# Context of the graph attention turned back by VectorE and DMA instead of TensorE, in a four-layer graph transformer on one core

## The reference

```python
h = jnp.maximum(_layernorm(x), 0.0);  x = x + attention(h, Wq, bq, Wk, bk, Wv, bv, Wf, bf, adj)
h = jnp.maximum(_layernorm(x), 0.0);  x = x + graph(h, adj, W, b, w_src, w_dst, H_w, H_b)

def graph(feat_in, adj, W, b, w_src, w_dst, H_w, H_b):     # 12 heads, 32 features each
    h = jnp.einsum('bnd,ade->bane', feat_in, W)
    th = jnp.tanh(h)
    attn = einsum('bane,aeo->bano', th, w_src) + swapaxes(einsum('bane,aeo->bano', th, w_dst), 2, 3)
    attn = jnp.where(attn >= 0, attn, 0.2 * attn)
    attn = softmax(jnp.where(~adj[:, None], -999.0, attn))
    feat_out = elu(heads_joined(jnp.einsum('banm,bame->bane', attn, h) + b))
    gate = sigmoid(feat_in @ H_w.T + H_b)
    return gate * feat_out + (1.0 - gate) * feat_in
```

## Time and profile before

| | |
|---|---|
| runs | 2123.85, 2126.32, 2125.83 us |
| the profiled execution | 2124.53 us, span 2122.7 us |
| TensorE matmuls, weight loads | busy 2035.4 us (96%), 1897.6 us (89%) |
| ScalarE, VectorE, GpSimd | busy 1954.5 (92%), 1779.6 (84%), 1570.1 us (74%) |
| granted TensorE clock | 0.991 of full speed over the span |
| DMA | 80.27 MB, mean 38 GB/s |

### The profile page before, as it was taken

The page is one execution under the profiler, slowest core; times in us unless marked ns, Lnnn a source line. Parts: engine busy times, 40 slices in busy tenths (PEclk is TensorE's granted clock), DMA queues, the critical chain, the costliest instruction groups (busy, mean ns, idle before and its releaser), DMA issues.

```text
span 2122.7 us, 58492 instructions
## 1 busy us (share of the span) xinstructions
PE 2035.4 (96%) x19980; PEld 1897.6 (89%) x19980; DVE 1779.6 (84%) x4117; ACT 1954.5 (92%) x6800; POOL 1570.1 (74%) x2874
## 2 busy tenths in 40 slices
PE   4999999999999999999999999999999999999985
PEld 3899889898899999999999999999999999999974
DVE  3688888888888888888888888888888888888876
ACT  3699899998999999999999999999999999999986
POOL 6467777777777777777777777777777777777765
PEclk9999999999999999999999999999999999999987
DMA  4001111111211000000320101001000010000000
GB/s 153 16 25 36 40 54 51 36 51 44 60 56 36 29 29 25 29 28 25 99 92 29 29 24 30 28 27 32 25 28 29 25 33 25 29 29 20 18 12 23
DMA packets 85983, 80.27 MB, mean 38 GB/s; under 512 B 22582, under 2 KB 85436, under 8 KB 85692
## 3 DMA queue, kind: packets, MB, share of 16 engines
q1 hardware_dynamic: 85692, 76.52, 11.8%
HBM read 44.26 MB, written 32.24 MB: 36 GB/s over the span
## 4 chain that ended last, share of the span: by engine, by line
PE 86%; POOL 8%; ACT 2%; issue 2%; DVE 1%; SPq 0%; DMA 0%; POOLq 0%; DVEq 0%; ACTq 0%
PE psum L718 36%; PE psum L728 18%; PE psum L710 5%; PE psum L796 5%; PE psum L807 4%; PE psum L818 4%; PE psum L784 3%; PE psum L854 2%; PE psum L741 2%; PE psum L836 2%; PE psum L750 2%; POOL prod L406 2%; PE psum L825 1%; POOL x L420 1%; POOL x L382 1%
## 5 line engine op out<-in xcount | busy, mean ns | idle before, releaser
L492 ACT ACTIVATE LG<-LG,neg_max 128x128 f32<-128x128 f32 x1536 | 602.1, 415 | 6.9 <-DVE neg_max L624 6.9
L492 ACT ACTIVATION_READ_ACCUMULATOR LG<-LG,neg_max 128x1 f32 x1536 | 328.6, 214 | 0.0
L486 ACT ACTIVATE LA<-LA,neg_max 128x128 f32<-128x128 f32 x768 | 297.8, 408 | 0.4 <-DVE neg_max L648 0.4
L406 POOL TENSOR_TENSOR prod<-th,vec 128x384 f32<-128x384 f32 x256 | 256.1, 1021 | 55.7 <-ACT th L533 55.7
L402 POOL TENSOR_TENSOR ey<-ey,hG 128x384 f32<-128x384 f32 x128 | 130.8, 1022 | 207.2 <-ACT ey L527 207.2
L620 DVE COPY_PREDICATED_SCALAR LG<-no_edge,no_edge_score 128x1536 f32 x128 | 253.5, 1981 | 24.7 <-ACT LG L524 23.8
L624 DVE TENSOR_REDUCE neg_max<-LG 128x12 f32<-128x1536 f32 x128 | 224.4, 1753 | 14.4 <-DVE LG L620 0.9
L728 PE MATMUL psum<-hT_hi,qk_lo 128*128 128x256 f32 x1152 | 199.7, 281 | 0.0
L728 PE MATMUL psum<-hT_hi,qk_hi 128*128 128x256 f32 x1152 | 199.0, 281 | 0.6 <-DVE hT_lo L595 0.4
L728 PE MATMUL psum<-hT_lo,qk_hi 128*128 128x256 f32 x1152 | 199.0, 282 | 0.0
L718 PE MATMUL psum<-hg_hi,gT_hi 128*128 128x384 f32 x768 | 195.6, 363 | 0.8 <-DVE gT_lo L599 0.8
(11 more groups left out here) (127 smaller groups left out, 6400.5 us busy)
## 6 DMA issues: line engine op xcount, KB each, us to landing
xin<-x SPq DMA_DIRECT2D x64, 192.0 KB, 2.4
x_mid<-x SPq DMA_DIRECT2D x64, 192.0 KB, 1.9
xin<-x_mid SPq DMA_DIRECT2D x64, 192.0 KB, 2.4
out<-x SPq DMA_DIRECT2D x64, 192.0 KB, 1.9
stage<-w_vf SPq DMA_DIRECT2D x8, 288.0 KB, 3.8
stage<-w_qk SPq DMA_DIRECT2D x12, 192.0 KB, 4.1
stage<-w_hg SPq DMA_DIRECT2D x8, 288.0 KB, 5.4
ahead<-ahead_hi SPq DMA_DIRECT2D x8, 288.0 KB, 3.4
```

The costliest lines, as they stand in the source:

```text
L406: last = pool.tensor_tensor(prod[:, i, :], th[:], vec[:, r.pair(k - 2), 2 + i, :], ALU.mult)
L486: last = act.activation(head, head, ACT.Exp, scale=-1.0, bias=neg_max[:, 0, h:h + 1], accum_out=rsum[:, h:h + 1])
L492: last = act.activation(head, head, ACT.Exp, bias=neg_max[:, 1, a:a + 1], accum_out=den[:, a:a + 1])
```

## The change

**The context.** `features(gcT, bank(5))` is gone from TensorE, and bank 5 is no longer waited for on its account. VectorE's copy becomes `dve.transpose`, which turns each 32x32 block of bank 7. The blocks themselves have to change places too: SP writes them to `context` in DRAM, four DMAs with runs of 32 floats, and one DMA loads the result to the new tile `back`. `y` is made from `back` one step later, so the stages behind it move by one step (k-5 to k-6, k-6 to k-7), the store as well; `HELD` and the gate's buffers go from 4 to 5, and the pipeline has one more step at its end.

**Orders.** VectorE: `hv` ahead of the transpose, then `cT_lo`, `sdR`, `y`, `hT_lo`. GpSimd: `neg_bias` to the place behind `no_edge`; the layernorm of k-1 ahead of `x` + bias; the score parts ahead of `x1` + `hG`. On TensorE the transposes of `hM` and of heads 8 to 11 move from the end of a step to the start of the next, which alters nothing in its order. SP: the round through DRAM stands ahead of the masks and the load of `x`; the reloads of `V` and `gate` change places.

**Side work.** The head biases are made at k = 0 and 2. A piece is split in two steps, the copy in one and the subtraction in the next, both behind `x` + bias; the high part goes to a free `stage` slot instead of `ahead_hi`.

```diff
 # SP
+            def context_back(g):
+                b = g % 2
+                sp.wait_ge(s["gc"], g + 1)
+                if g >= 1:
+                    sp.wait_ge(s["pv_norm"], g)
+                rows = context[b].rearrange("(i b) (r q a) -> q b r i a", b=32, q=4, a=32)
+                for q in range(4):
+                    sp.dma_start(rows[q], gcT[32 * q:32 * q + 32, :].rearrange("p (r i a) -> p r i a", r=KC, i=4)).then_inc(s["gc_out"], 16)
+                sp.wait_ge(s["gc_out"], 64 * (g + 1))
+                sp.dma_start(back[:], context[b]).then_inc(s["gc_back"], 16)
...
+                g = k - 5
+                if 0 <= g < ALL:
+                    context_back(g)
 # GpSimd
+                split_ahead(k)
...
             def setup(k):
-                if k in (-3, -2):
-                    pool.wait_ge(s["hb_in"], 16 * PAIRS)
-                    pool.wait_ge(s["ident_in"], 16)
-                    head_bias(k - (-3))
+                for pair, at in ((0, 0), (1, 2)):
+                    if k == at:
+                        pool.wait_ge(s["hb_in"], 16 * PAIRS)
+                        pool.wait_ge(s["ident_in"], 16)
+                        head_bias(pair)
 # VectorE
                 if r.has(k - 5):
+                    if r.has(k - 6):
+                        dve.wait_ge(s["gc_out"], 64 * r.done(k - 6))
                     dve.wait_ge(s["gc_ps"], r.done(k - 5))
-                    dve.tensor_copy(gcT[:], bank(7)[:, 0:D]).then_inc(s["gc"], 1)
+                    dve.transpose(gcT[:], bank(7)[:, 0:D]).then_inc(s["gc"], 1)
...
-                if r.has(k - 5):
-                    dve.wait_ge(s["pv_rden"], r.done(k - 5))
-                    dve.wait_ge(s["pv_ps"], r.done(k - 5))
...
+                if r.has(k - 6):
+                    dve.wait_ge(s["pv_rden"], r.done(k - 6))
+                    dve.wait_ge(s["gc_back"], 16 * r.done(k - 6))
...
 # TensorE
-                if r.has(k - 4):
-                    pe.wait_ge(s["gc"], r.done(k - 4))
-                    wait_latest(pe, r, ("s_max", k + 2), ("qk2", k + 3), ("z_leaky", k - 3), ("pv_norm", k - 5))
-                    features(gcT, bank(5)).then_inc(s["pv_ps"], 1)
```

More of the change, by code:

```diff
@@ L43 @@
 QK_ORDER = [0, 3, 1, 4, 2, 5]
-FIRST_STEP, STEPS_BEHIND = -5, 6
-HELD = 4
+FIRST_STEP, STEPS_BEHIND = -5, 7
+HELD = 5
 STAGES = 8
@@ L129, in graph_stack @@
         gcT = sb("gcT", [128, D])
+        back = sb("back", [128, D])
         y = sb("y", [128, D])
@@ L329, in straight @@
                                  ).then_inc(stored[slot], 16)
-            for k in range(-3, ALL + 6):
+                if k == B + 1:
+                    sp.wait_ge(s["g_gate_ps"], B)
+                    load_next("gate")
+            for k in range(-3, ALL + 7):
                 straight(k)
@@ L377, in step @@
             def step(r, k):
[L378 to L381 removed]
+                if r.has(k - 7):
+                    b = (k - 7) % SLOTS
+                    pool.wait_ge(s["mixed"], r.done(k - 7))
+                    pool.wait_ge(s["xf"], r.done(k - 7))
                     pool.tensor_tensor(x1[:, b, :], y[:], x1[:, b, :], ALU.add).then_inc(s["x2"], 1)
@@ L392, in step @@
                     pool.tensor_scalar(no_edge[:, (k - 2) % 2, :], adj8[:, (k - 2) % SLOTS, :], -1.0, 1.0, ALU.mult, ALU.add).then_inc(s["masks"], 1)
+                if r.has(k + 2):
+                    pool.wait_ge(adj_in[(k + 2) // HALF_SLOTS % 2], r.dma(k + 2))
+                    wait_latest(pool, r, ("s_max", k))
+                    pool.tensor_scalar(neg_bias[:, (k + 2) % 2, :], adj8[:, (k + 2) % SLOTS, :], -1.0, -NEG, ALU.add, ALU.mult).then_inc(s["bias_mask"], 1)
+                if r.has(k - 1):
+                    layernorm(r, "g", 1, k - 1)
                 if r.has(k):
@@ L524, in step @@
                     act.activation(LG[:].rearrange("p (e n) -> p e n", e=3), banks(4, 3), ACT.Prelu, alpha=SLOPE).then_inc(s["z_leaky"], 1)
-                if r.has(k - 5):
-                    act.wait_ge(s["y_min"], r.done(k - 5))
+                if r.has(k - 6):
+                    act.wait_ge(s["y_min"], r.done(k - 6))
                     act.activation(ey[:], ey[:], ACT.Exp).then_inc(s["y_exp"], 1)
@@ L736, in step @@
             def step(r, k):
+                if r.has(k + 4):
+                    pe.wait_ge(s["m_h"], r.done(k + 4))
+                    wait_latest(pe, r, ("g_haug", k - 3), ("m_lo", k + 3))
+                    features(hM, bank(2)).then_inc(s["m_hT"], 1)
                 if r.has(k - 4):
+                    pe.wait_ge(s["z_exp2"], r.done(k - 4))
+                    wait_latest(pe, r, ("cT_lo", k), ("gpt2", k - 5))
+                    for a in range(8, 12):
+                        last = pe.transpose(bank(0)[:, (a % 4) * N:(a % 4 + 1) * N], LG[:, a * N:(a + 1) * N], idf[:])
+                    last.then_inc(s["gpt_ps2"], 1)
                     pe.wait_ge(s["z_exp0"], r.done(k - 4))
@@ L845, in step @@
                     features(hG[:, (k - 1) % HELD, :], bank(1)).then_inc(s["g_hT"], 1)
-                if r.has(k + 5):
-                    pe.wait_ge(s["m_h"], r.done(k + 5))
-                    wait_latest(pe, r, ("g_haug", k - 2), ("m_lo", k + 4))
-                    features(hM, bank(2)).then_inc(s["m_hT"], 1)
-                if r.has(k - 3):
-                    pe.wait_ge(s["z_exp2"], r.done(k - 3))
-                    wait_latest(pe, r, ("cT_lo", k + 1), ("gpt2", k - 4))
-                    for a in range(8, 12):
-                        last = pe.transpose(bank(0)[:, (a % 4) * N:(a % 4 + 1) * N], LG[:, a * N:(a + 1) * N], idf[:])
-                    last.then_inc(s["gpt_ps2"], 1)
             def setup(k):
```

135 lines of the change are left out of this document (64 added, 71 removed).

## The result

The changed kernel takes 2072.52 us (median of four runs, 2070.91 to 2074.19) against 2124.94 for the kernel before on the same chip: a ratio of 0.9753, 95% interval 0.9736 to 0.9770. That is 52.4 us less. The forecast was 2058, so the gain came out 14.5 us smaller. The stated range of 2046 to 2084 held; the forecast's own, 2050 to 2068, did not. The profiled execution took 2070.91 us with a span of 2069.1 us, 53.6 less than before's 2122.7; the sum had promised 67.7.

A forecast was written before the change was run, and what follows sets the result against it. TensorE's queue was taken as the bound, 15.69 us a step, with ScalarE 0.5 below. 38.9 + 21.4 + 11.2 - 3.8 = 67.7 us off gave a median of 2058 us, chance 0.58; range 2046 to 2084, the forecast's own 2050 to 2068.

The forecast's parts named there:

- Part 1, the period: The context's three transposes leave TensorE: step 15.69 to 15.36 us, 119 steps, gain 38.9 us.
- the two loops of ScalarE and VectorE: ScalarE alone at 15.23 us and ScalarE-VectorE-ScalarE through the leaky ReLU at 15.34, both under TensorE's 15.36.
- Rival (a): ScalarE and VectorE become the bound in the middle, 15.53 us a step: 2078 us, chance 0.19.
- its sign, TensorE waiting in each step: ScalarE's hole ahead of `th` gone and TensorE waiting for ScalarE or VectorE in each step.
- Part 2, VectorE's order: The transpose takes the copy's 0.55 us, may be 0.5 longer before TensorE notices; steady step neither gains nor loses.
- Rival (e): VectorE's transpose takes several passes, 2.2 us, 1.15 beyond the cover: slower, 2195 us, chance 0.04.
- Part 3, the way through DRAM: The context's round from `y` to the next `y` takes 7 to 11 us, hidden in a step up to 14.8.
- Rival (d): The round through DRAM outlasts the step: slower, 2200 us at a 16 us round, chance 0.05.
- Part 4, the splits: Weight splits on GpSimd make `hM` late, 24.4 us of stalls; halves cost 3, gain 21.4 us.
- no waits of TensorE for `hM` from 112 us on: A sign that the forecast is right: after the start, TensorE never waits for GpSimd's `hM`.
- Part 5, the start: Moving the head biases gains 19 us; a 6.3 us hole at step 2 and 1.5 of slower matmuls leave 11.2.
- Part 6, the end: The last `y` comes 5.8 us later through DRAM, 2 saved in the steps ahead: loss 3.8 us.

The follow-up runs named there:

- experiment 10: On experiment 1, VectorE makes the 32x32 transpose twice, the first time into a spare tile: 2079.84 us, ratio 0.9785.
- experiment 9: On experiment 1, the scatter of the context to DRAM issued and waited for twice: 2081.43 us; four times: 2750.45 us (one execution).
- experiment 1: The changed kernel with GpSimd's `x` + bias put back ahead of the layernorm of k-1: 2062.31 us, ratio 0.9710.
- experiment 8: On experiment 1 with head bias 1 in gaps, each weight piece's subtraction divided, two of three chunks ahead of the first `ey`: 2049.86 us, ratio 0.9645.
- experiment 3: The kernel before with GpSimd's order, head biases and split halves alone: 2089.88 us; the same with `x` + bias ahead of the layernorm: 2092.24 us.
- Experiments 5 and 7: 5: changed kernel, head biases back at k = -3 and -2, 2083.51 us; 7: experiment 1, head bias 1 in two parts in GpSimd's gaps, 2053.83 us.
- Experiment 4: The changed kernel with GpSimd's old order, head biases and splits, so the context's way alone on the kernel before: 2123.49 us, ratio 0.9998.

## Why the prediction was right or wrong

**Part 1, the period: mechanism right, floor not.** TensorE's new period is 15.365, to the hundredth, wherever TensorE sets it. The sum took 15.36, because the two loops of ScalarE and VectorE that it looked at lay under it. A third, through the attention's exponentials and VectorE's product, was not looked at. It had room, until the product's 959 ns became 1469 by a swap that no part of the sum mentions; then it took 15.41, which is 3.6 us over the run. Rival (a) came true in kind, at 0.05 us a step where I had priced it at 0.17, and from another cause; its sign, TensorE waiting in each step, was seen in part.

**Part 2, VectorE's order: right.** The transpose takes 0.57 us at 0.50 from start to start; one place, `cT_lo`, had 0.35 of cover instead of 0.5, which only a second transpose laid bare (experiment 10). Rival (e) did not occur.

**Part 3, the way through DRAM: right.** 6.5 us, a little under the 7 to 11 of the prediction; no step of the middle waits for it. Rival (d) would need a round of more than twice the length (experiment 9).

**Part 4, the splits: the mis-sized term.** 21.4 forecast, 12.7 measured. It failed at "a 1.42 subtraction delays by 0.45 ... I charge 3 us". The subtraction took 2.16, because it began behind an addition that had held up the product, which then held it up; that is 3.9 of the missing 8.7 (experiment 1 brings them back). The other 4.8 stay without the swap: the push of `ey` and `hG` was 0.7 us instead of 0.2 to 0.3, 0.47 of it `shift` beside the product (experiment 8). At the old period, where each step has 0.33 us more, the stalls went but for 0.6 us (experiment 3): the gains of parts 1 and 4 draw on the same room, and I had added them. The prediction's sign "no waits of TensorE for `hM` from 112 us on" failed in a small way too: 22 waits, 5.7 us in all, none over 0.4. One input erred the other way: `neg_bias` takes 0.54 us at its old place, beside a product of VectorE, and 0.30 at the new one, so it fills 0.4 us of GpSimd's gap and not 0.6.

**Part 5, the start: right.** The hole came where it was foreseen, 6.6 us ahead of an `hM` from 60 us on. Experiments 5 and 7 confirm both sides, 11.0 for moving the biases and 8.5 more for the hole that they left. The 1.5 us missing in the table are within the scatter of the starts.

**Part 6, the end: right in size, partly by luck.** -2.7 against -2.5 with the four steps in it; the chain was as foreseen, but the same end differs by up to 3 us from one kernel to the next.

**The interplay.** `neg_bias` moved out of the stretch ahead of `hM` looked like a detail of part 4. Experiment 4 shows that without the side work the context's part is worth 0.8 us, no more than the noise; it put back GpSimd's order, the biases and the splits together, so it doesn't single out `neg_bias`. The prediction had the cause in its numbers (0.10 of cover against 0.33) but not in its sum, where 38.9 stands as TensorE's own.

## What to carry to other kernels

When a change moves work on GpSimd, lay its timeline beside VectorE's: where a VectorE instruction with two inputs in SBUF met a wide GpSimd instruction here, the later of the two stood still until the earlier was all but done. A duration read before a move holds only for what stood beside it. When the bound falls by 0.3 us a step, take the cover of every feeder again before adding gains: here one part alone gave 0.8 us, the other 32.0, both 63.3. The loop through DRAM with one buffer cost nothing in the middle at 7.2 and 11.2 us of a step of 15.4, but the steps at the end of the program are shorter (7 to 12 us), and there it is paid per step.

## What the runs showed of the hardware

- VectorE's product on 128x768 in SBUF (0.96 us alone) beside GpSimd's addition on 128x384: 1.12 with 0.30 us of overlap, 1.47 with 0.65. It ends 0.82 after the addition in both. `y` (0.55 alone) ends 0.41 after a subtraction of GpSimd. In each case the instruction is done its own length less 0.14 us after the other's end. GpSimd's `rstd` on 128x1 (0.57 us) is an exception: a product that starts second and overlaps it by 0.50 us keeps its 0.96.
- GpSimd in turn: `shift` on 128x1, 0.27 us alone, 0.74 to 0.78 beside the product; `neg_bias` on 128x128 0.30 and 0.54; the copy of 128x576, which reads one tile, 0.66 and 1.40; the subtraction 1.43 and 2.16. GpSimd's addition that came first keeps its 1.01.
- VectorE's 32x32-block transpose of 128x384 float32 out of PSUM: 0.57 us, as a copy of the same tile. Two in a row start 0.50 apart.
- A scatter of 192 KB from SBUF to DRAM as 1536 runs of 128 B, in four DMAs of SP: 0.62 us an issue, landed 4.04 us after the first issue; each DMA of 48 KB 2.1 us from issue to landing, the load back 2.4. Ordinary stores of 192 KB land in 1.9.
